# A fused attention and expert network on one core: row norms by a power on GpSimd, and a third buffer for the router's rows

## The reference

```python
def _layernorm(x, axis=-1, eps=1e-05):
    m = jnp.mean(x, axis=axis, keepdims=True)
    v = jnp.var(x, axis=axis, keepdims=True)
    return (x - m) / jnp.sqrt(v + eps)

x = x + _L0_attn_a_ref(_layernorm(x, axis=-1), ...)   # causal attention without a softmax, 16 heads of 8
x = x + _L0_ffn_ref(_layernorm(x, axis=-1), ...)      # 16 experts, each row goes to its best 2, with a capacity
x = x + _L0_attn_b_ref(_layernorm(x, axis=-1), ...)   # attention for the 6 best queries of each head
x = x + _L0_ffn_ref(_layernorm(x, axis=-1), ...)
return x
```

## Time and profile before

| what | us |
|---|---|
| times of three runs | 1787.49, 1797.24 (median), 1805.49 |
| span of the profiled execution, first to last instruction | 1549.5 |
| median less span | 247.7 |
| busy: PE | 1305.2 (84% of the span) |
| busy: DVE | 1137.9 (73%) |
| busy: ACT | 768.2 (50%) |
| busy: POOL | 732.2 (47%) |

### The profile page before, as it was taken

The page is one execution under the profiler, slowest core; times in us unless marked ns, Lnnn a source line. Parts: engine busy times, 40 slices in busy tenths (PEclk is TensorE's granted clock), DMA queues, the critical chain, the costliest instruction groups (busy, mean ns, idle before and its releaser), DMA issues.

```text
span 1549.5 us, 28769 instructions
## 1 busy us (share of the span) xinstructions
PE 1305.2 (84%) x8534; PEld 802.8 (52%) x8534; DVE 1137.9 (73%) x5084; ACT 768.2 (50%) x1903; POOL 732.2 (47%) x1041
## 2 busy tenths in 40 slices
PE   3988888887899999999999999999999989999300
PEld 1555554454798964444444444444444448888300
DVE  3898998898473658788888889888888784755422
ACT  2343443341564766555655656556555556646200
POOL 2135555446423213354555655545554342347775
PEclk9999999999899988888988979978888889999755
DMA  6645412001354520000000000110000003557522
GB/s 171 226 140 176 139 57 75 27 24 55 112 187 155 176 83 14 10 19 26 22 23 28 29 21 21 38 60 28 29 25 18 28 29 121 162 159 229 161 80 70
DMA packets 119770, 125.82 MB, mean 81 GB/s; under 512 B 15552, under 2 KB 109888, under 8 KB 119616
## 3 DMA queue, kind: packets, MB, share of 16 engines
q1 hardware_dynamic: 103232, 90.42, 18.2%
q0 software_dynamic: 16384, 33.59, 7.5%
HBM read 50.15 MB, written 73.79 MB: 80 GB/s over the span
## 4 chain that ended last, share of the span: by engine, by line
PE 49%; DVE 27%; issue 7%; POOL 7%; ACT 5%; DMA 3%; SPq 1%; POOLq 0%; ACTq 0%; DVEq 0%
PE pair L1814 19%; DVE pT L1321 7%; PE pair L1741 7%; POOL vmyg L522 5%; DVE pT L1047 3%; PE pair L1752 3%; DVE xs L1231 3%; PE pair L1730 2%; PE pair L1605 2%; ACT pT L816 2%; PE bank L1544 2%; PE bank L1550 2%; PE bank L1842 2%; DVE st L898 2%; PE bank L1802 1%
## 5 line engine op out<-in xcount | busy, mean ns | idle before, releaser
L1814 PE MATMUL pair<-kT,apart 32*128 32x512 f32 x2048 | 480.6, 743 | 34.7 <-DVE smax L1321 33.4
L816 ACT ACTIVATE pT<-pair 128x256 f32<-128x256 f32 x1024 | 328.9, 396 | 259.0 <-PE pair L1814 257.5
L1321 DVE CUSTOM_DVE_ANT_0 pT<-pair,pT 128x256 f32<-128x256 f32 x1024 | 381.4, 417 | 100.9 <-ACT pT L816 97.4
L1814 PEld LDWEIGHTS pair<-kT,apart 32*128 32x128 f32 x2048 | 196.0, 210 | 194.7 <-DVE smax L1321 118.9
L1741 PE MATMUL pair<-xeT,unit_w 128*128 128x256 f32 x768 | 186.9, 387 | 0.0
L1047 DVE TENSOR_TENSOR pT<-pair,causal 128x512 f32<-128x512 f32 x256 | 158.4, 680 | 23.8 <-PE pair L1605 23.8
L522 POOL DMA_INDIRECT vmyg<-ybufA,slg x128 | 122.3, 955 | 84.9 <-issue 36.6
L1206 DVE TENSOR_TENSOR hid<-sg,pair 128x512 f32<-128x512 f32 x96 | 65.9, 686 | 126.3 <-ACT sg L742 125.9
L1741 PEld LDWEIGHTS pair<-xeT,unit_w 128*128 128x128 f32 x768 | 142.0, 195 | 16.0
L482 POOL DMA_INDIRECT dispB<-xnf,sli x128 | 126.5, 988 | 43.6 <-issue 43.6
L482 POOL DMA_INDIRECT dispA<-xnf,sli x128 | 126.9, 992 | 40.6 <-issue 40.6
(11 more groups left out here) (235 smaller groups left out, 2025.8 us busy)
## 6 DMA issues: line engine op xcount, KB each, us to landing
dispB<-zeros SPq DMA_DIRECT2D x16, 1408.0 KB
apart<-dispA SPq DMA_DIRECT2D x96, 128.0 KB
ybufA<-ye SPq DMA_DIRECT2D x48, 256.0 KB
apart<-dispB SPq DMA_DIRECT2D x96, 128.0 KB
ybufB<-ye SPq DMA_DIRECT2D x48, 256.0 KB
dispA<-zeros SPq DMA_DIRECT2D x33, 128.0 KB
xs<-in_x SPq DMA_DIRECT2D x16, 256.0 KB, 3.0
out<-xs SPq DMA_DIRECT2D x16, 256.0 KB, 2.5
```

Source lines behind the costliest of these rows:

```text
L816: act.activation(rel[n % RING][:, q, :], pair[n % RING][:, q, HALF:SEQ], ACT.Relu).then_inc(s["relu_done"], 1)
L1321: dve.tensor_tensor_reduce(out=rel[n % RING][:, q, :], in0=pair[n % RING][:, q, 0:HALF], in1=rel[n % RING][:, q, :], scale=1.0, scalar=LOW ...
L1814: pe.matmul(pair[n % RING][:, q, :], apart[h][at, j, t * P:(t + 1) * P], kTs[h][at, HALF:], start=True, stop=True).then_inc(s["bsc_done"], 1)
```

## The change

DVE's part of a row norm ends with the aggregates. POOL gets a function `norm_scale` that computes `rstd` by one power with the exponent -0.5, and `nmr` from it: four small operations a call, of which the power waits for the first and the last for the power. `norm_scale` stands in POOL's order in attention A between `send(b-3)` and `places(b-2)`, in attention B between `send(b-2)` and `normed(b-1)`. DVE waits for the moments of the call before when it takes new statistics, and for `rstd_ready` of the call before when it takes new aggregates. The router's rows get a third buffer; `sent` and `xnf_free` go, and the users of `xnf` wait for the sends of three batches before. `places` waits for the sends of two batches before, since it writes their index list.

```diff
+NF = 3
...
-        lnh = sb("lnh", [P, 2 * TB])
-        lny = [sb(f"lny{h}", [P, 2 * TB]) for h in range(2)]
-        lnt = sb("lnt", [P, 2 * TB])
-        lnu = sb("lnu", [P, 2 * TB])
+        mhalf = sb("mhalf", [P, 2 * TB])
+        negm = sb("negm", [P, 2 * TB])
...
-        xnf = [sb(f"xnf{h}", [P, TB, D]) for h in range(2)]
+        xnf = [sb(f"xnf{r}", [P, TB, D]) for r in range(NF)]
...
             def places(b, g, h):
 
                 cols = slice(b * TB * K, (b + 1) * TB * K)
                 pool.wait_ge(s["rk_done"], g + 2)
+                if g >= 2:
+
+                    pool.wait_ge(s[f"sent{h}"], 16 * TB * K * (g // 2))
...
-            def sent(i, h):
-
-                pool.wait_ge(s[f"sent{h}"], (i + 1) * 16 * TB * K)
-                pool.sem_inc(s["xnf_free"], 1)
+            def norm_scale(call, W):
+
+                pool.wait_ge(s["moments"], call + 1)
+                if call < CALLS:
+
+                    pool.wait_ge(s["att_xn_ready"], min(call, B))
+                    pool.wait_ge(s["ffn_xn_ready"], max(call - 3, 0))
+                else:
+                    pool.wait_ge(s["ffn_xn_ready"], B)
+                pool.tensor_scalar(lnv[:, 0:W], mv[:, 0:W, 1], EPS, None, ALU.add).then_inc(s["rs"], 1)
+                pool.tensor_scalar(negm[:, 0:W], mv[:, 0:W, 0], -1.0, None, ALU.mult)
+                pool.wait_ge(s["rs"], 2 * call + 1)
+                pool.tensor_tensor(rstd[:, 0:W], lnv[:, 0:W], mhalf[:, 0:W], ALU.pow).then_inc(s["rs"], 1)
+                pool.wait_ge(s["rs"], 2 * call + 2)
+                pool.tensor_tensor(nmr[:, 0:W], negm[:, 0:W], rstd[:, 0:W], ALU.mult).then_inc(s["rstd_ready"], 1)
...
                 if b >= 3:
                     send(b - 3, (b - 3) // 2, 1 - h)
-                    sent((b - 3) // 2, 1 - h)
+                norm_scale(b + 2, norm_width(b))
                 if before:
                     places(b - 2, b - 2, h)
 
+            norm_scale(0, TB)
             pool.wait_ge(s["vm_zero"], 1)
             for c in range(TB):
                 masked_v(0, 0, c, True)
+            norm_scale(1, TB)
             each_batch_b(pool, attention_a)
             send(B - 3, B // 2 - 2, 1)
-            sent(B // 2 - 2, 1)
+            norm_scale(B + 2, TB)
...
             def normed(b, n, dst, kind, q, call):
 
                 pool.wait_ge(s["rstd_ready"], call + 1)
+                if kind == "ffn":
+
+                    pool.wait_ge(s[f"sent{(n - NF) % 2}"], 16 * TB * K * ((n - NF) // 2 + 1))
...
                 if before:
                     places(b - 2, b - 2 + B, h)
                     send(b - 2 + B, u - 1 + B // 2, h)
-                    sent(u - 1 + B // 2, h)
+                norm_scale(b + 2 + CALLS, norm_width(b))
                 if last:
-                    normed(b - 1, b - 1 + B, xnf[1 - h], "ffn", 0, b + 2 + CALLS)
+                    normed(b - 1, b - 1 + B, xnf[(b - 1 + B) % NF], "ffn", 0, b + 2 + CALLS)
...
-                if kind == "ffn":
-
-                    act.wait_ge(s["xnf_free"], n + 1)
+                if kind == "ffn" and n >= NF:
+
+                    act.wait_ge(s[f"sent{(n - NF) % 2}"], 16 * TB * K * ((n - NF) // 2 + 1))
...
             def row_stats(call, batches):
+                if call:
+
+                    dve.wait_ge(s["moments"], call)
...
             def row_aggregates(call, W):
                 dve.wait_ge(s["stats"], call + 1)
+                if call:
+
+                    dve.wait_ge(s["rstd_ready"], call)
...
-            def row_moments(call, W):
...
-            def first_guess(call, W):
...
-            def newton(call, W, steps):
...
-            def row_shift(call, W):
...
-                row_moments(call, W)
-                newton(call, W, range(3))
-                row_shift(call, W)
+                row_aggregates(call, W)
                 if next:
                     k_and_v(b + 1, 1 - h, 0)
...
-                    if last and n == 0:
-                        last_newton(b - 1)
...
-                    if n == 29:
-                        call = b + 2 + CALLS
-                        if last:
-                            row_aggregates(call, TB)
-                        first_guess(call, norm_width(b))
-                    if n in (30, 31):
-                        newton(b + 2 + CALLS, norm_width(b), (n - 30,))
-                if not next:
-                    last_newton(b)
+                    if last and n == 29:
+                        row_aggregates(b + 2 + CALLS, TB)
...
             def fetched_aggregates(b):
...
+                dve.wait_ge(s["rstd_ready"], b + 2 + CALLS)
```

More of the change, by code:

```diff
@@ L428, in _ @@
         def _(pool):
-            pool.sem_inc(s["xnf_free"], 2)
             pool.memset(ident[:, :], 0.0)
@@ L591, in _ @@
             fetch(1, 1)
-            for h in range(2):
-                sent(B // 2 - 1, h)
             def selected_rows(b):
@@ L643, in _ @@
             send(2 * B - 2, B - 1, 0)
-            normed(B - 1, 2 * B - 1, xnf[1], "ffn", 0, B + 2 + CALLS)
+            norm_scale(B + 2 + CALLS, TB)
+            normed(B - 1, 2 * B - 1, xnf[(2 * B - 1) % NF], "ffn", 0, B + 2 + CALLS)
             places(B - 1, 2 * B - 1, 1)
@@ L717, in attention_a @@
                 if last:
-                    apply_norm(b - 1, b - 1, xnf[1 - h], "ffn", 0, b + 2)
+                    apply_norm(b - 1, b - 1, xnf[(b - 1) % NF], "ffn", 0, b + 2)
                     turned(b - 1, "ffn", xfT)
@@ L764, in chain_a @@
                 if g == 3:
-                    apply_norm(B - 1, B - 1, xnf[1], "ffn", 0, B + 2)
+                    apply_norm(B - 1, B - 1, xnf[(B - 1) % NF], "ffn", 0, B + 2)
                 if g == 4:
@@ L925, in newton @@
-            def newton(call, W, steps):
-                for r in steps:
-                    y, z = lny[r % 2], (lny[1 - r % 2] if r < 2 else rstd)
-                    dve.wait_ge(s["rs"], call * 11 + 2 + 3 * r)
-                    dve.tensor_tensor(lnt[:, 0:W], y[:, 0:W], y[:, 0:W], ALU.mult).then_inc(s["rs"], 1)
-                    dve.wait_ge(s["rs"], call * 11 + 3 + 3 * r)
-                    dve.tensor_tensor(lnu[:, 0:W], lnt[:, 0:W], lnh[:, 0:W], ALU.mult).then_inc(s["rs"], 1)
-                    dve.wait_ge(s["rs"], call * 11 + 4 + 3 * r)
-                    dve.scalar_tensor_tensor(out=z[:, 0:W], in0=lnu[:, 0:W], scalar=1.5, in1=y[:, 0:W],
-                                             op0=ALU.add, op1=ALU.mult).then_inc(s["rs"], 1)
@@ L936, in row_shift, with norm @@
-            def row_shift(call, W):
-                dve.wait_ge(s["rs"], call * 11 + 11)
-                dve.scalar_tensor_tensor(out=nmr[:, 0:W], in0=mv[:, 0:W, 0], scalar=-1.0, in1=rstd[:, 0:W],
-                                         op0=ALU.mult, op1=ALU.mult).then_inc(s["rstd_ready"], 1)
-            def norm(call, *batches, parts=range(5)):
-                W = len(batches) * TB
-                if 0 in parts:
-                    row_stats(call, batches)
-                if 1 in parts:
-                    row_moments(call, W)
-                if 2 in parts:
-                    newton(call, W, (0,))
-                if 3 in parts:
-                    newton(call, W, (1,))
-                if 4 in parts:
-                    newton(call, W, (2,))
-                    row_shift(call, W)
+            def norm(call, *batches):
+                row_stats(call, batches)
+                row_aggregates(call, len(batches) * TB)
@@ L1249, in chain_a @@
                     residual_a(b)
+                    dve.wait_ge(s["moments"], B + 2)
                     batch_stats(0, b).then_inc(s["stats"], 1)
@@ L1255, in chain_a @@
                     route_counts(b - 1)
-                    row_moments(B + 2, TB)
-                if g == 2:
-                    newton(B + 2, TB, range(3))
-                    row_shift(B + 2, TB)
+                    row_aggregates(B + 2, TB)
                 if g == 3:
@@ L1296, in start_b @@
                     dve.wait_ge(s["combined"], 1)
-                    norm(CALLS, 0, parts=range(2))
-                if g == 8:
-                    norm(CALLS, 0, parts=range(2, 4))
-                if g == 9:
-                    norm(CALLS, 0, parts=(4,))
+                    norm(CALLS, 0)
                 if g == 12:
@@ L1304, in start_b @@
                     dve.wait_ge(s["combined"], 2)
-                    norm(CALLS + 1, 1, parts=range(2))
-                if g == 13:
-                    norm(CALLS + 1, 1, parts=range(2, 4))
-                if g == 14:
-                    dve.wait_ge(s["att_xn_ready"], B + 1)
-                    norm(CALLS + 1, 1, parts=(4,))
+                    norm(CALLS + 1, 1)
             experts(0, chain_a)
@@ L1451, in fetched_stats @@
                     dve.wait_ge(s["combined"], b + 3)
+                    dve.wait_ge(s["moments"], b + 2 + CALLS)
                 for j in ((2, 3) if second else (0, 1)):
@@ L1491, in pieces @@
                     residual(b)
```

(14 more changed lines are left out.)

29 lines of the change are left out of this document (8 added, 21 removed).

## The result

The change gave 8 us: 1784.11 us (median, 1775.09 to 1797.64) beside 1792.22 for the kernel before, ratio 0.996 with a 95% interval of 0.9941 to 0.998. Forecast were 1776 us and 21.5 us of gain. The time lies in the stated range of 1752 to 1805, but 13 of the 21.5 us are missing.

A forecast was written before the change was run, and what follows sets the result against it. PE held half the chain of waits and DVE a quarter, alternating in attention A. Terms 5.0 + 2.7 + 3.0 + 4.8 + 6 = 21.5 us off 1797.2 gave 1776 us; stated range 1752 to 1805, the forecast's own 1768 to 1785.

The forecast's parts named there:

- The time around the span: Whole kernel: the gain off the profile's span of 1549.5 us was carried over to the median of 1797.2 us.
- Attention A, steady batches: Attention A, 12 plain batches: norm hidden behind ACT's `apart`, only the idle 0.42 before `xnf` comes back; 5.0 us.
- The third buffer: Router's rows in A: ACT's 1.16 wait for landing goes, 1.2 plus about 1.5 us; nothing from two buffers in B.
- The start: First two norms of the kernel: 2.4 and 3.4 us each become 1.4, together 3.0 us gained.
- X = 0.6, near the lower row: Norm on POOL: the power over 8 columns takes 0.6 us, with bounds of 0.20 and 3.9.
- the slow-power rival: Power makes `rstd` later than today, in A from X = 1.65; 1807 us at 2.5, 1847 at 3.9; chance 0.13.
- is none: A's 17.38 us wait at 387.54 gives zero, because `norm_scale` stands behind POOL's eight sends.
- Attention B: 4.8 + 6: B: 16 batch ends at 0.3 give 4.8 us; every fifth of 15 batches turned quick, some 6, a judgement.
- The rival of a clock that comes back: Attention B: all batches become like the 43.3 us one, 31 us there, 42 in all, 1755 us; chance 0.15.
- POOL blocks DVE: New POOL operations each hold up a DVE operation of the chain, 46 us, 1822 us; chance 0.04.
- freed time is hidden: B's terms are absent and A gives half; some 8 us remain, 1789 us, no change; chance 0.20.

The follow-up runs named there:

- b0: The unchanged kernel before, run again for a second profile at the 1790 level: 1787.73 us, span 1785.3.
- f4: The unchanged kernel before, run again for its stages at the 1545 level: 1544.01 us, span 1541.9.
- f2: Against the kernel before, 1545 level: three Newton steps on VectorE in A, power on GpSimd in B, three buffers; 1528.5 us, ratio 0.9907.
- e2: Changed kernel with two buffers instead of three, norm by the power on GpSimd, against the kernel before: 1781.4 us, ratio 0.9959.
- b1: The unchanged kernel before, run once more at the 1790 level for the scatter of its stage times: 1792.24 us.
- f1: The whole change against the kernel before at the 1545 level: 1545.84 against 1543.44 us, ratio 0.9999.
- the first profile: Profile of the unchanged kernel before that the prediction rested on, from the 1545 level: span 1549.5 us.
- g1: Third buffer alone, norm left on VectorE with Newton steps, against the kernel before at the 1545 level: 1530.18 us, ratio 0.9897.

## Why the prediction was wrong

**The time around the span.** "247.7 us is what the median has around that span (start and end of the program)", and with it "carried over to the median one to one": this failed first. Profiles with a time of their own have 2 to 3 us around the span (1781.11 less 1779.1, 1544.01 less 1541.9; the largest is 3.3, in two runs). The 247.7 was two levels. At the upper one pauses are part of the time, 6 us in each batch of A, and a sum made in a trace without them doesn't hold there. The spans of b0 and f4 differ by 243 us, and the idle time of PE that ends in "issue" makes 78 of them; how the rest comes about was not followed.

**Where the 13 us went.** At the 1790 level, where the forecast was measured, the terms were A's steady batches 5.0, the third buffer 2.7, the start 3.0 and B 10.8. Measured there: the start about 2, the rest of A nearly 6 us of loss (its end is 3.7 later in all), the buffer 0, B 11.6. That adds to 8, the measured gain. The two terms that failed are the steady batches, by the power's length (without the power A ends 9 us earlier), and the buffer.

**The power.** "X = 0.6, near the lower row", was 1.68, inside the bounds 0.20 to 3.9 but just past the threshold of the slow-power rival ("it decides from X = 1.65"). The threshold itself holds: the doubled power shows a full price above it, the multiply-add only a part below it.

**Attention A, steady batches: 5.0 us forecast.** The mechanism stood where the norm is short. At the 1545 level batches are 21.65 apart with three Newton steps, 21.12 with two and 21.11 with the multiply-add, so 0.53 of the norm's length was to be had, near the 0.42 of the earlier trace rows; and nothing is left from then on, since `apart` and `xnf` follow each other on ACT. With X = 1.68 it is 21.78, 0.13 worse. What I had left out was the clock in A: three batches 3.0 us longer, 9 of the 12.8 us that A's end is behind f2's (407.4 and 394.6). Why it falls more often there is not shown. At the 1790 level the change costs A 3.7 us (means of the ends, 470.4 and 466.7) instead of giving 5; of this e2's 466.7 shows nothing, so the 3.7 is near the scatter, but the 5 us are not there in any profile with the power.

**The third buffer: 2.7 us.** At the 1790 level 0 (1.0011): the pauses leave the sends time to land, and POOL waited for them once from 100 to 440 in b0, 3.3 us, and not at all in b1, instead of seven times; the batch of ACT's first wait, which the term rests on, is no longer than its neighbours. At the 1545 level that batch gives 2.1, near the 2.7, and the buffer 15 in all. The statement that the wait near 387 "is none" was right for the whole change and for the reason given: `norm_scale` stands behind eight sends, and f1's `xnf` still starts at 395.47. With the buffer alone that wait is a prize, of 7.8 us. The other 5 of the 15 have no row: in f4 two falls of the clock make 2.7 of them, and the first profile, whose A ends 5 us earlier, has no such falls.

**The start: 3.0 us.** The third `nmr` of the start came 2.7 us earlier (45.81 against 48.51), the fifth 2.1 (87.08 against 89.21), so two thirds of this term held. The first norm gave 0.3 instead of 1.0 (15.28 against 15.59), since with 4 columns its power takes 1.045.

**Attention B: 4.8 + 6.** B gave 11.6 us at the 1790 level against 10.8 forecast. That the size held is in part luck: it was worked out from a trace of the other level, the 6 of it were a judgement, and nothing shows that it came in the shares I gave. At the 1545 level the power in B adds nothing that a measurement shows (0.9907 with it, 0.9897 without, both with the buffer), although that is the level of the earlier trace rows. The granted clock from 900 to 1250 was 0.82 before (0.79 in b1) and 0.82 after, and at the 1545 level 0.84 and 0.87 before and 0.85 after, so "batches turned quick by the clock" is not shown. The rival of a clock that comes back is out at both levels.

**POOL blocks DVE** did not happen on the scale that rival needed (46 us): the 494 instructions gone, at 0.169 us each 83 us, took 72 off DVE's busy time, so at most 11 went into slower ones. The rival "freed time is hidden" named the nearest time (1789, 8 us of gain) with the opposite shares: B's terms are what remained, and A's are what is missing. The Trainium skill's GPSIMD Engine Reference, under Performance versus the Vector engine, holds that elementwise work is about twice as dear on GpSimd; this case's small operations agree weakly (0.20 and 0.23 against 0.17), and the power is 8 times a product of the same shape.

**The better kernel.** Third buffer, Newton steps on VectorE in A and the power on GpSimd in B is equal to the changed kernel at the 1790 level (0.996) and 1.1% quicker at the other (1528.5 against 1545.84). At the 1545 level the two-step kernel (0.9861 and 0.9879) and the buffer alone (0.9897) stand close to it.

## What to carry to other kernels

Hold a profile's span against that execution's own time before you build on it, and if only other runs' times are at hand, take a gap of a sixth for a different state of things, not for something around the program. Where a chain moves to another engine, find the length at which the next engine's own work stops hiding it, and measure the one unknown instruction against that length: here 1.68 against 1.65 left nothing of the 0.5 us a batch that a short norm gives. And count the batches in which the clock fell before you compare the same stage of two profiles: a fall made a plain batch 1.3 to 3.0 us longer here, and the unchanged kernel had one of them in one profile and three in the next.

## What the runs showed of the hardware

- A GpSimd power takes 1.68 us for 128x8 and 1.045 for 128x4, where a product of 128x8 takes 0.20.
- The same program has two levels of time, 1545 and 1790 us, on the same chip, with pauses of TensorE's issue of 0.3 to 1.1 us between single matmuls at the upper one (38.7 us on the values line alone against 0.0), and with like idle time on VectorE (100 us against 0) and ScalarE (65 against 2). On TensorE they stand where GpSimd's indirect DMAs run; whether these cause them is not shown.
- The granted clock fell to 0.50 behind idle spells of TensorE of 1.03 us and less. Of f1's batches with spells of 1.03 and 0.69, 0.6 of work between them, 6 of 12 were followed by it; of those of the unchanged kernel with 0.78 and 0.69, 1.8 of work between, two in f4 and none in g1. So the same spells are followed by it in some batches and not in others.
